# A graph layer on one core: unread products, later diagonal blocks and three doubled adjacency loads

## What is computed

```
h    = relu(layernorm(x))                     x: 8 x 2048 x 128, float32
S    = relu((A + A^T) / 2)                    A: 2048 x 2048, float32
D    = sum of S by rows;  d = D^-0.5 (0 where D = 0)
L    = I - d S d
out  = x + relu(L (h W))                      W: 128 x 128
```

## Time and profile before

| | before |
|---|---|
| median of 3 runs | 403.52 us (403.36 to 403.84) |
| the profiled execution | 404.02 us |
| its span, first to last instruction | 402.2 us |
| outside the span | 1.8 us |
| PE busy | 376.3 us, 94% of the span |
| DVE busy | 314.6 us, 78% |
| ACT busy | 190.0 us, 47% |
| mean granted TensorE clock | 0.975 |
| chain that ended last | PE 84%, DVE 6%, DMA 4%, SP's queue 4% |

### The profile page before, as it was taken

The page is one execution under the profiler, slowest core; times in us unless marked ns, Lnnn a source line. Parts: engine busy times, 40 slices in busy tenths (PEclk is TensorE's granted clock), DMA queues, the critical chain, the costliest instruction groups (busy, mean ns, idle before and its releaser), DMA issues.

```text
span 402.2 us, 6113 instructions
## 1 busy us (share of the span) xinstructions
PE 376.3 (94%) x2121; PEld 202.1 (50%) x2121; DVE 314.6 (78%) x606; ACT 190.0 (47%) x408; POOL 121.2 (30%) x260
## 2 busy tenths in 40 slices
PE   4378869999999999999999999999999999999995
PEld 3368754444444444545454445444544554454454
DVE  2875989797999797999969579967975796679246
ACT  1466986979976777777744124312201221113001
POOL 0599305397698235654311120400000000000000
PEclk9686998999999999999999999999999999999999
DMA  8999999101146322341344039921140123012203
GB/s 248 369 386 387 387 281 267 35 27 55 53 145 193 134 81 67 118 157 52 106 147 142 26 96 322 338 82 52 33 125 2 52 66 93 0 54 78 80 27 106
DMA packets 69567, 55.00 MB, mean 137 GB/s; under 512 B 2848, under 2 KB 58272, under 8 KB 69536
## 3 DMA queue, kind: packets, MB, share of 16 engines
q1 hardware_dynamic: 69536, 54.60, 42.6%
HBM read 39.91 MB, written 14.68 MB: 136 GB/s over the span
## 4 chain that ended last, share of the span: by engine, by line
PE 84%; DVE 6%; DMA 4%; SPq 4%; issue 1%; ACT 0%; DVEq 0%
PE ps L1197 14%; PE ps L1196 14%; PE ps L1202 14%; PE ps L1212 10%; PE ps L1214 10%; PE ps L1213 10%; DMA S<-in_adj_dram 4%; PE ps L1126 2%; DVE S L797 2%; SPq L450 2%; SPq L431 2%; PE ps L1249 2%; PE ps L1250 2%; PE ps L1248 2%; PE ps L1153 2%; PE ps L1172 1%
## 5 line engine op out<-in xcount | busy, mean ns | idle before, releaser
L1196 PE MATMUL ps<-S,hbuf 128*128 128x512 f16 x240 | 91.0, 379 | 0.0
L1197 PE MATMUL ps<-S,hbuf 128*128 128x512 f16 x240 | 91.0, 379 | 0.0
L1202 PE MATMUL ps<-S,hbuf 128*128 128x512 f16 x256 | 76.1, 379 | 0.0
L1212 PE MATMUL ps<-S,hbuf 128*128 128x512 f16 x152 | 57.6, 379 | 0.0
L1213 PE MATMUL ps<-S,hbuf 128*128 128x512 f16 x152 | 57.6, 379 | 0.0
L1214 PE MATMUL ps<-S,hbuf 128*128 128x512 f16 x152 | 57.6, 379 | 0.0
L716 ACT ACTIVATE g<-ps 128x512 f16<-128x512 f32 x31 | 18.2, 595 | 68.5 <-DVE ps L896 32.0
L816 DVE SCALAR_TENSOR_TENSOR S<-S,dneg 128x512 f16<-128x512 f32 x54 | 42.7, 805 | 3.9 <-ACT S L677 3.4
L658 ACT ACTIVATE ps<-hbuf,lnt 128x128 f32<-128x128 f32 x104 | 41.7, 449 | 5.1 <-DVE hbuf L789 5.1
L677 ACT ACTIVATE S<-S,dneg 128x512 f16<-128x512 f32 x54 | 37.8, 717 | 5.5 <-DVE S L816 4.9
L1202 PEld LDWEIGHTS ps<-S,hbuf 128*128 128x128 f16 x256 | 25.1, 98 | 30.1
(11 more groups left out here) (141 smaller groups left out, 703.2 us busy)
## 6 DMA issues: line engine op xcount, KB each, us to landing
S<-in_adj_dram SPq DMA_DIRECT2D x15, 1024.0 KB, 14.4
hbuf<-in_x_dram SPq DMA_DIRECT2D x64, 128.0 KB, 3.1
sums<-in_x_dram SPq DMA_DIRECT2D x32, 256.0 KB, 2.8
out_dram<-sums SPq DMA_DIRECT2D x31, 256.0 KB, 2.5
t_forms<-work SPq DMA_DIRECT2D x24, 256.0 KB, 2.9
S<-t_forms SPq DMA_DIRECT2D x5, 1024.0 KB, 9.6
S<-in_adj_dram SPq DMA_DIRECT2D x2, 512.0 KB, 12.3
S<-t_forms SPq DMA_DIRECT2D x1, 768.0 KB, 10.7
```

The costliest lines, as they stand in the source:

```text
L1196: nc.tensor.matmul(acc, hbuf[:, u, 0, at:at + P], l_hi(t), start=(i == 0), stop=False)
L1197: nc.tensor.matmul(acc, hbuf[:, u, 1, at:at + P], l_hi(t), start=False, stop=False)
L1202: last = nc.tensor.matmul(acc, hbuf[:, u, 0, at:at + P], l_lo(t), start=False, stop=(i == T - 1))
L1212: nc.tensor.matmul(acc, a_hi, b_hi, start=starts, stop=False)
```

## The change

- **Loads.** A list `loads` takes the place of the loop over `steps`. Blocks (1, 0) and (1, 1), (2, 0) and (2, 1), (3, 0) and (3, 1) are each one transfer of 2 MiB whose rows are 4 KB long, with one semaphore for both blocks. So (1, 1) comes with (1, 0), (2, 1) before (1, 2), and (3, 1) before (1, 3). W goes behind the first block. Units 4 and 5 of x go behind the transfer of (1, 0) and (1, 1).
- **Unread products.** PE no longer waits for DVE's last mirror but for the first add of the last step (`a_added`), and multiplies into bank 0: 12 products before the turn of the maximum, 7 after it.
- **ACT.** In the last step the first mirror of step 8 is taken before the first relu of step 9.
- **Diagonal blocks.** `row_tiles` begins with 8 to 13, then 0 to 5. Nothing of the diagonal stands in the degree chain; four blocks are done behind the low parts 2 to 5, four more in the first four turns of the main loop. The wait for `h_lo` follows the first use of each unit.

```
-IDLE_TURNS = (6, 8)
+IDLE_TURNS = (12, 7)
...
-    x_step = [0, 0, 0, 0, 1, 1]
+    loads = [(0, 0, 1), (0, 1, 2), (1, 0, 2), (0, 2, 3), (2, 0, 2), (1, 2, 3), (0, 3, 4), (3, 0, 2), (1, 3, 4), (2, 2, 3), (2, 3, 4), (3, 2, 3), (3, 3, 4)]
+    x_load = [0, 0, 0, 0, 2, 2]
...
-        row_tiles = list(range(EARLY)) + list(range(UNITS, UNITS + EARLY)) + [m for m in range(T) if m % UNITS >= EARLY]
+        row_tiles = list(range(UNITS, UNITS + EARLY)) + list(range(EARLY)) + [m for m in range(T) if m % UNITS >= EARLY]
...
-        adj_in = [[sem(f"adj_in{i}_{j}") for j in range(G)] for i in range(G)]
+        adj_in = [[None] * G for i in range(G)]
+        for i, j0, j1 in loads:
+            adj_in[i][j0:j1] = [sem(f"adj_in{i}_{j0}")] * (j1 - j0)
...
-            sp.dma_start(w_raw, w).then_inc(w_in, 16)
-            for s, (i, j) in enumerate(steps):
-                load_adj(i, j)
-                if i < j:
-                    load_adj(j, i)
+                    sp.dma_start(S[:, GRP * i + k0:GRP * i + k1, j * WIDE:j1 * WIDE],
+                                 adj_v[i][:, k0:k1, j * WIDE:j1 * WIDE]).then_inc(done, 16)
+
+            for s, (i, j, j1) in enumerate(loads):
+                load_adj(i, j, j1)
+                if s == 0:
+                    sp.dma_start(w_raw, w).then_inc(w_in, 16)
                 for u in range(EARLY):
-                    if x_step[u] == s:
+                    if x_load[u] == s:
                         load_x(u)
...
                 for k in range(GRP):
-                    relu_s(s, k)
+                    if s < len(steps) - 1 or k:
+                        relu_s(s, k)
                     for p in mirrors_at[s]:
                         if k not in DVE_MIRRORS[pairs.index(p)]:
                             take_mirror(p, k)
+                    if s == len(steps) - 1 and k == 0:
+
+                        relu_s(s, k)
...
             nc.vector.tensor_tensor(t, dsafe[:], y, ALU.mult).then_inc(deg_chain, 1)
-            take_diag(0)
             dve.wait_ge(max_turned, 1)
...
                     for t in range(LEAD):
-                        take_diag(t + 1)
                         split_l_lo(t)
+                        if t >= LEAD - GRP:
+                            take_diag(t - (LEAD - GRP))
...
-                if tau < HALF - LEAD - 1:
-                    take_diag(tau + LEAD + 1)
+                if tau < GRP:
+                    take_diag(GRP + tau)
...
-            pe.wait_ge(m_taken_dve, sum(len(ks) for ks in DVE_MIRRORS))
+            pe.wait_ge(a_added, GRP * (len(steps) - 1) + 1)
             pe.wait_ge(h_hi_ready, 1)
-            keep_busy(7, IDLE_TURNS[0])
+            keep_busy(0, IDLE_TURNS[0])
             pe.wait_ge(max_ready, 1)
             nc.tensor.transpose(ps[:, 4, 0:P], gmax[:, 0:1].to_broadcast([P, P]), ident[:]).then_inc(max_turned, 1)
-            keep_busy(7, IDLE_TURNS[1])
+            keep_busy(0, IDLE_TURNS[1])
...
-                if s % 2 == 0 and mt < UNITS:
+                if s % 2 == 0 and row_tiles.index(mt % UNITS) + row_tiles.index(mt % UNITS + UNITS) > 2 * i:
+
                     wait_h_lo(pe, u + 1)
```

More of the change, by code:

```diff
@@ L443, in store_sums, with load_adj @@
                              sums[:, e % SUMS, :].rearrange("p (i f) -> p i f", i=GRP)).then_inc(out_done[e % SUMS], 16)
-            def load_adj(i, j):
+            def load_adj(i, j, j1):
                 whole = (i, j) != steps[-1]
@@ L449, in load_adj @@
                     k1 = GRP if whole else k0 + GRP // 2
-                    sp.dma_start(S[:, GRP * i + k0:GRP * i + k1, j * WIDE:(j + 1) * WIDE],
-                                 adj_v[i][:, k0:k1, j * WIDE:(j + 1) * WIDE]).then_inc(done, 16)
-            sp.dma_start(w_raw, w).then_inc(w_in, 16)
-            for s, (i, j) in enumerate(steps):
-                load_adj(i, j)
-                if i < j:
-                    load_adj(j, i)
+                    sp.dma_start(S[:, GRP * i + k0:GRP * i + k1, j * WIDE:j1 * WIDE],
[4 more added lines that the diff above has]
+                    sp.dma_start(w_raw, w).then_inc(w_in, 16)
                 for u in range(EARLY):
-                    if x_step[u] == s:
+                    if x_load[u] == s:
                         load_x(u)
```

## The result

The changed kernel took 404.96 us (median of 22 runs), the kernel before 403.88 us in 22 runs beside them. The ratio is 1.0025, 95% interval 1.0014 to 1.0035: slower by 1.0 us (1.1 by the medians), small but clear of no change. The forecast was 404.7 us, +1.2. The profiled execution took 404.79 us with a span of 403.0, so its span is 0.8 us longer than that of before.

A forecast was written before the change was run, and what follows sets the result against it. PE was taken as the bound from its first product, so that product's start decides. Front +2.3 us and end -1.1 us gave +1.2 on 403.52, so 404.7 us, range 402.0 to 406.0.

The forecast's parts named there:

- The sum: Whole kernel: front +2.3 us and end -1.1 us make +1.2 us, 404.7 us.
- the front: Stretch before PE's first product: +2.3 us in all, bounds 1.5 and 3.2.
- PE carries the front to the end: From its first product PE is the bound; a microsecond won or lost ahead of it is one of the whole time.
- Order of the loads: Front: new order and merged blocks move step 5 to 39.0 from 38.00; step 1 about 18, step 3 27.5, step 4 31.0.
- Long rows: Loads in the front: 4 KB rows save 0.9 us in all over three doubled transfers, bounds 0 and 1.0.
- W's place: Loads in the front: W behind the first block saves 0.3 us, bounds 0 and 0.4.
- The low clock at step 5: Front: after 4.4 us without work step 5 starts at the low clock, so step 6 starts at 45.1, +2.2 us.
- What stands behind step 6: Rest of the front: step 8's 0.24 us wait taken up, 0.3 us added for ACT's late mirrors.
- The end: End of the front, degree chain to first product: 3.07 us against 4.15, -1.1 us, bounds -0.8 and -1.3.
- Unit 7: DVE ends it at 80.38, product 13 wants it at 80.5: 0.1 us of room, cost 0, bounds 0 and 0.4.
- The clock stays up: Rival in the front: step 5 runs at the high clock, front even, end's 1.1 us stays: 402.4 us, chance 0.27.
- the case that had been given 0.50: The forecast itself: step 5 at the low clock, 404.7 us, spanning 403.7 to 405.9, chance 0.50.

The follow-up runs named there:

- the filled gap: The changed kernel with 14 unread products in PE's idle time before step 5: 402.87 us, ratio 0.9968 against the kernel before.
- before filled: The kernel before with unread products in PE's idle time before step 4 (12) and step 6 (5): 404.27 us, ratio 1.0007.
- the loads alone: The kernel before with only the new loads (order, doubled transfers, W behind the first block): 405.56 us, ratio 1.0042.
- the 2 KB version: The changed kernel with each doubled transfer issued as two of 1 MiB with 2 KB rows: 405.44 us, ratio 1.0031 against the kernel before.
- the version with the third pair split: The changed kernel with (3,0) and (3,1) as two transfers in the old order: 402.00 us, ratio 0.9958 against the kernel before.

## Why the prediction was right, point by point

- **The sum.** Forecast +2.3 - 1.1 = +1.2, in the traces +1.98 - 1.21 = +0.77: the front 0.3 too dear, the end 0.1 too small a gain, both to the same side. That 404.7 lies so near to the measured 404.96 has some luck in it, since the base of 403.52, a median of three runs, was 0.36 below that of 22.
- **PE carries the front to the end.** Right: first product +0.77, span +0.8, no new wait behind it.
- **Order of the loads.** Step 5 forecast at 39.0, found at 38.93 (its idle time ended by "issue" in the view, not by the DMA); step 1 at 18 (17.62), step 3 at 27.5 (27.23), step 4 at 31.0 (30.88).
- **Long rows.** 0.9 us in all: the starts give 1.1, the time 0.9, and the rate 410 GB/s where 0.17 us less for 1 MiB meant 414. The three cycles for each packet in the Trainium skill, page "DMA: Bandwidth & Descriptors", section "Why small descriptors are slow (HBM only)", would make 2.2% by an estimate. The prediction left out that the same section has 32 bytes of metadata for each operation besides, by an estimate 0.8% more. The windows show 5.9% (387 to 410), so the measurement goes beyond both together.
- **W's place.** Put at 0.3, not shown. Since step 5 came right, part of what I gave to W belongs to the rows.
- **The low clock at step 5.** Right, and shown to be the whole loss of the front by the filled gap. It was mis-sized by 0.3: turns and mirrors took 5.84 us (38.93 to 44.77) and not 6.14, as the clock came back at about 43.6. What stands behind step 6 was +0.1 (1.87 to 1.98), where I had 0.06; the wait on ACT is there (0.94 at 51.27), but the filled kernel has it too (0.93 at 49.35), so it does not come from the low clock.
- **The end.** -1.21 against -1.1; the reduction began 1.08 us behind the chain's start (63.71) where it had been 1.36, so the lost diagonal block gave 0.28 and not 0.2. What I did not see is how little of the whole is certain. The 0.9 us of clock in it was there to gain in two of the three traces with the old end (before, and before filled) and not in the third (the loads alone). I took the fall of the clock in one execution for a property of the kernel. And I had put the diagonal blocks at 0.2 in all: where the clock does not fall, they also stand in front of the first low part, another 0.2.
- **Unit 7.** Ended at 82.05 (81.36 + 0.69 in the timeline of DVE), wanted at 65.57 + 13 x 1.29 = 82.3. No wait, with 0.3 us of room.
- **The rivals.** "The clock stays up" was a real one: an execution of the 2 KB version ran that way, and one of the 22 runs of the changed kernel, at 402.45, lies where this rival put it (402.4); it has no trace. The other 21, from 404.12 to 405.66, fit the case that had been given 0.50.

## What to carry to other kernels

When transfers are merged or reordered, compute for each consumer the byte position at which its last operand lands; the merged kernel can move the same bytes sooner and still be slower. Look at each idle stretch that this opens on TensorE and at the clock behind it: here 4.3 us without work cost nothing by themselves and 2.1 us through the clock. Fill such a stretch with unread products or with a step whose data is already there, before judging the merge. Filling gains only where the slower turns make something late: in the kernel before, step 6 waited for its data in any case and the time stayed the same. And take more than one trace of a stretch in which the clock falls, before putting its price into a sum.

## What the runs showed of the hardware that was not expected

- An idle stretch of the same length was followed by a fall of the clock in one trace and not in another. The 2.05 us at the end of the front were followed by one in the traces of before and of before filled, and not in that of the loads alone. So were the 2.1 us behind a stretch of 1.7 in the version with the third pair split; but not the 2.65 us ahead of step 5 of before filled (its turns took 1.94 us) nor the 2.91 with 2 KB rows. The stretches of 4.08 to 4.47 us ahead of step 4 or 5 always were, in the five traces that have one. Whether the work ahead of the stretch or chance decides in between, no run here separates.
- With the long rows, the runs of the changed kernel filled lay within 0.4 us (402.57 to 402.99), against 3.2 us in its 22 runs unfilled (402.45 to 405.66) and 3.3 us in those of before (403.01 to 406.26). But with W first or with 2 KB rows the filled kernel still scattered by 2 us, and the loads alone, with nothing filled, by only 1.0 (405.08 to 406.03). So the clock of these gaps is not shown to be what scatters the runs.
- Rows of 4 KB load at 410 GB/s where rows of 2 KB load at 387, on an otherwise equal queue.
